# The last two batches of a switch-head attention layer on one core: DVE adds gated heads with fused multiply-adds, and the last batch is turned, projected and stored per token tile

## What is computed

```python
gl_v = (x @ Ws).reshape(b, t, h, e)
wv = _topk_mask(gl_v, SEL) * jax.nn.sigmoid(gl_v)
xv = jnp.einsum('btd,edk->btek', x, Wv)
v = jnp.einsum('bthe,btek->bhtk', wv, xv)
...
attn = jnp.einsum('bhij,bhjd->bihd', probs, v)
gl_o = (x @ Wd).reshape(b, t, h, e)
mask_o = _topk_mask(gl_o, SEL)
out = jnp.einsum('bthe,bthk,ekd->btd', mask_o, attn, Wo)
```

## Time and profile before

| | us |
|---|---|
| median of 3 executions | 2942.46 |
| lowest, highest | 2939.79, 2952.21 |
| the profiled execution | 2944.26 |
| its span | 2942.5 |
| mean granted TensorE clock | 0.88 |

### The profile page before, as it was taken

One profiled execution on the slowest core, in us unless ns is written; L12 is line 12 of the kernel. 1 busy time (PEld: TensorE's weight loads), 2 busy tenths in 40 slices (PEclk: granted clock), 3 DMA queues, 4 the chain that ended last, 5 costly groups with the idle time before them and its releaser, 6 DMA issues. The chain is left out here.

```text
span 2942.5 us, 31726 instructions
## 1 busy us (share of the span) xinstructions
PE 2436.2 (83%) x10259; PEld 1141.4 (39%) x10259; DVE 1903.9 (65%) x3077; ACT 1689.0 (57%) x2384; POOL 1925.0 (65%) x1920
## 2 busy tenths in 40 slices
PE   5567787877778877755998999999999999999995
PEld 2222333333333332223554454444444444444433
DVE  5798979798888797721332555656565565646554
ACT  1788888888888789920222545454444544444350
POOL 5656577778687778856774027566767574756685
PEclk8678777789787777776999999999999999999996
DMA  2000000000100000164996000000000000000000
GB/s 99 15 1 8 10 15 17 15 17 15 17 15 17 15 10 15 17 113 108 282 261 134 1 1 1 1 15 8 15 8 15 8 1 22 1 8 1 8 1 15
DMA packets 92453, 99.00 MB, mean 34 GB/s; under 512 B 20320, under 2 KB 88032, under 8 KB 92256
## 3 DMA queue, kind: packets, MB, share of 16 engines
q1 hardware_dynamic: 66544, 69.80, 9.0%
q0 software_dynamic: 25712, 26.90, 4.7%
HBM read 69.98 MB, written 26.67 MB: 33 GB/s over the span
## 5 line engine op out<-in xcount | busy, mean ns | idle before, releaser
L944 POOL TENSOR_TENSOR TT<-TT,SS 128x512 f32<-128x512 f32 x512 | 649.8, 1305 | 218.8 <-ACT SS L874 218.3
L1644 ACT ACTIVATE PR<-S,NM 128x512 f32<-128x512 f32 x512 | 347.0, 683 | 492.7 <-DVE NM L1812 492.6
L1812 DVE TENSOR_REDUCE NM<-S 128x2 f32<-128x1024 f32 x256 | 313.0, 1223 | 294.7 <-PE S L1548 293.9
L447 PE MATMUL OB<-TT,VAL 128*17 128x512 f32 x1024 | 339.8, 766 | 53.6 <-ACT TT L882 53.5
L700 DVE TENSOR_SCALAR TT<-SC 128x1024 f32<-128x1024 f32 x256 | 311.6, 1217 | 81.4 <-PE SC L426 49.1
L949 POOL DMA_INDIRECT slot_tokens<-TID,IDX x256 | 258.9, 1011 | 138.0 <-issue 79.2
L702 DVE SCALAR_TENSOR_TENSOR SS<-SC,TT 128x1024 f32<-128x1024 f32 x256 | 313.6, 1225 | 20.6 <-issue 1.8
L1577 PE MATMUL OT<-TT,VN 128*64 128x512 f32 x1024 | 278.8, 623 | 20.7 <-ACT TT L1650 16.8
L1548 PE MATMUL S<-TT 64*128 64x512 f32 x1024 | 292.1, 646 | 0.7 <-ACT TT L1613 0.7
L1559 PEld LDWEIGHTS TP<-ident,PR 128*128 128x128 f32 x2048 | 227.1, 141 | 149.8 <-issue 121.1
L1559 PE MATMUL TP<-ident,PR 128*128 128x128 f32 x2048 | 275.5, 278 | 10.1 <-DVE TT L1817 8.7
(11 more groups left out here) (272 smaller groups left out, 4168.2 us busy)
## 6 DMA issues: line engine op xcount, KB each, us to landing
TT<-w_gu SPq DMA_DIRECT2D x64, 384.0 KB, 3.9
TT<-w_dn SPq DMA_DIRECT2D x64, 128.0 KB, 4.2
XL<-x SPq DMA_DIRECT2D x8, 512.0 KB, 4.0
rows<-XL SPq DMA_DIRECT2D x8, 512.0 KB, 10.2
slot_tokens<-TID,IDX POOLq DMA_INDIRECT x256
TT<-w_dn SPq DMA_DIRECT2D x64, 64.0 KB, 4.9
XS<-stream SPq DMA_DIRECT2D x8, 512.0 KB, 3.8
out<-XS SPq DMA_DIRECT2D x8, 512.0 KB, 2.9
```

Source lines behind the costliest of these rows:

```text
L447: ins = pe.matmul(OB[r:r + DH0 + 1, :], values_of[:, mt, h, :], TT[:, h % RING, mt, :], start=(mt == 0), stop=(mt == NT - 1))
L944: ins = pool.tensor_tensor(tt[:, mt, :], tt[:, mt, :], ss[:, mt, :], ALU.add)
L1644: act.activation(PR[s % 2][h2][:], S[s % 2][:, h2, :], ACT.Exp, bias=NM[:, s % 2, h2:h2 + 1], accum_out=SM[:, pair % 2, j, h2:h2 + 1]).the ...
L1812: dve.tensor_reduce(NM[:, s % 2, :], S[s % 2][:], AX, ALU.max, negate=True).then_inc(sems["peak"], 1)
```

## The change

It has three parts.

1. **Lending.** DVE takes both heads of pair 3 of batch 6 over from POOL. `lend` 0 and 1 stand at steps 8 and 9 of run 15: for each token tile and expert one `scalar_tensor_tensor` of 128x64 that multiplies a head's output with one column of choices and adds it to GO, so 20 for each head. POOL's `gate` for that pair is gone, and in its place POOL waits for `lent` and counts `gadd` up by two. PE waits for `lent` ahead of `turn_out2` 0.
2. **Fused gating of the last batch.** DVE's even heads of pairs 1 and 2 are added with 20 such instructions each instead of 4 products (L1752) and an addition (L1756). For pair 0 the 4 products stay. Of pair 3 DVE now takes both heads, and POOL none.
3. **Tile by tile at the end.** In place of `join`, three `turn_out2` and four `product_out2` there is `finish` for each token tile: DVE adds the 10 fused instructions of pair 3 and joins the tile (128x320), PE turns it in 3 transposes, ACT copies it (128x384), PE makes the product one tile later in its queue, DVE adds the residual, and SP stores 128 KB. Ahead of the first tile PE has 4 products of 128x512 into a bank that nobody reads.

```diff
--- before.py
+++ after.py
@@ -1179,15 +1179,14 @@
 OUT_2_LATE = table((0, 12, 1, "turn_out2", 0), (0, 13, 1, "turn_out2", 1), (0, 13, 2, "turn_out2", 2),
                    (0, 14, 1, "product_out2", 0), (0, 14, 2, "product_out2", 1), (0, 15, 2, "product_out2", 2),
                    (1, 0, 1, "product_out2", 3))
-OUT_2_TAIL = table((0, 4, 3, "join", 0), (0, 4, 3, "turn_out2", 0), (0, 4, 3, "turn_out2", 1), (0, 4, 3, "turn_out2", 2),
-                   (0, 4, 4, "product_out2", 0), (0, 4, 4, "product_out2", 1), (0, 4, 4, "product_out2", 2),
-                   (0, 4, 4, "product_out2", 3))
+OUT_2_TAIL = table(*[(0, 4, 3, "finish", j) for j in range(NT + 1)], *[(0, 4, 4, "residual", j) for j in range(NT)])
 HEADS_1 = table((0, 7, 1, "spread", 0), (0, 11, 1, "spread", 1), (0, 15, 1, "spread", 2), (1, 3, 1, "spread", 3),
                 (0, 7, 2, "heads1", 0), (0, 11, 2, "heads1", 1), (0, 15, 2, "heads1", 2), (1, 3, 2, "heads1", 3))
 HEADS_2 = table((0, 7, 2, "set_down", 0), (0, 11, 2, "set_down", 1), (0, 15, 2, "set_down", 2), (1, 3, 2, "set_down", 3),
                 (0, 8, 2, "heads2", 0), (0, 12, 2, "heads2", 1), (1, 0, 2, "heads2", 2), (1, 4, 2, "heads2", 3),
                 (0, 9, 3, "gate", 0), (0, 13, 3, "gate", 1), (1, 3, 3, "gate", 2), (1, 7, 3, "gate", 3))
-HEADS_2_TAIL = HEADS_2[:8] + table((0, 9, 3, "gate", 0), (0, 13, 3, "gate", 1), (1, 0, 3, "gate", 2), (1, 4, 3, "gate", 3))
+HEADS_2_TAIL = HEADS_2[:8] + table((0, 9, 3, "gate", 0), (0, 13, 3, "gate", 1), (1, 0, 3, "gate", 2))
+LEND = table((1, 8, 3, "lend", 0), (1, 9, 3, "lend", 1))
 
 
 def timetable():
...
@@ -1200,6 +1199,8 @@
 
     for r, (kind, b) in enumerate(RUNS):
         put(r, HEADS_1 if kind == 1 else HEADS_2 if b < B - 2 else HEADS_2_TAIL, b)
+        if (kind, b) == (2, B - 2):
+            put(r, LEND, b)
         if r + 1 == TAIL:
             put(r, OUT_2_LATE, b - 1)
             continue
...
@@ -1344,13 +1345,16 @@
                 sp.dma_start(X[b][:], x_b[b]).then_inc(sems[f"x_in{b}"], 16)
             for dst, src in loads_later:
                 sp.dma_start(dst, src).then_inc(sems["weights_later"], 16)
-            for b in range(B):
+            for b in range(B - 1):
                 sp.wait_ge(sems["x4"], b + 1)
                 sp.dma_start(out_b[b], X[b % XN_RING][:]).then_inc(sems["out_st"], 16)
                 if b + XN_RING < B:
                     sp.wait_ge(sems["out_st"], 16 * (b + 1))
                     sp.dma_start(X[b % XN_RING][:], x_b[b + XN_RING]).then_inc(sems[f"x_in{b % XN_RING}"], 16)
-            sp.wait_ge(sems["out_st"], 16 * B)
+            for j in range(NT):
+                sp.wait_ge(sems["row_out"], j + 1)
+                sp.dma_start(out_b[B - 1][:, j, :], X[(B - 1) % XN_RING][:, j, :]).then_inc(sems["out_st"], 16)
+            sp.wait_ge(sems["out_st"], 16 * (B - 1 + NT))
 
         @block.tensor
         def _(pe):
...
@@ -1488,26 +1492,40 @@
                 ins.then_inc(sems["item_d"], 1)
 
             def turn_out2(v, c, b):
-                last = b == B - 1
-                bank = free_bank(c) if last else item(v, "free_d")
-                if last and c == 0:
-                    pe.wait_ge(sems["joined"], 1)
-                elif c == 0:
-                    pe.wait_ge(sems["gadd"], v.next("gadd", H1))
+                bank = item(v, "free_d")
+                if c == 0:
+                    pe.wait_ge(sems["gadd"], v.next("gadd", H1) - (2 if b == B - 2 else 0))
+                    if b == B - 2:
+                        pe.wait_ge(sems["lent"], 2)
                 lo = min(c * P, SV - P)
                 for j in range(NT):
-                    ins = pe.transpose(bank[:, j * P:(j + 1) * P], (GL_POOL if last else GO)[:, j, lo:lo + P], ident[:])
+                    ins = pe.transpose(bank[:, j * P:(j + 1) * P], GO[:, j, lo:lo + P], ident[:])
                 ins.then_inc(sems["item_d"], 1)
 
-            def product_out2(v, j, b):
-                bank = free_bank(3 + j) if b == B - 1 else item(v, "free_d")
-                if b == B - 1 and v.all_due("free_d"):
-                    pe.wait_ge(sems["free_d"], v.value + 3)
+            def out2_into(bank, j):
                 for c in range(3):
                     r = 0 if c < 2 else 3 * P - SV
                     ins = pe.matmul(bank[:, 0:D], AT2[r:P, c, j * P:(j + 1) * P], o2[r:P, c, :],
                                     start=(c == 0), stop=(c == 2))
-                ins.then_inc(sems["item_d"], 1)
+                return ins
+
+            def product_out2(v, j, b):
+                out2_into(item(v, "free_d"), j).then_inc(sems["item_d"], 1)
+
+            def finish(v, i, b):
+
+                if i == 0:
+                    for _ in range(4):
+                        pe.matmul(free_bank(6), ident[:], q2[:, 0, :], start=True, stop=True)
+                if i < NT:
+                    pe.wait_ge(sems["joined"], i + 1)
+                    for c in range(3):
+                        lo = min(c * P, SV - P)
+                        ins = pe.transpose(free_bank(i)[:, c * P:(c + 1) * P], GL_POOL[:, i, lo:lo + P], ident[:])
+                    ins.then_inc(sems["turned_j"], 1)
+                if i > 0:
+                    pe.wait_ge(sems["down_j"], i)
+                    out2_into(free_bank((4, 5, 6, 0)[i - 1]), i - 1).then_inc(sems["done_j"], 1)
 
             def spread(v, pair, b):
 
...
@@ -1613,6 +1631,12 @@
                     act.activation(dst(i, b), src(), ACT.Copy, scale=scale).then_inc(sems["free_a"], 1)
                 return run
 
+            def finish(v, i, b):
+                if i < NT:
+                    act.wait_ge(sems["turned_j"], i + 1)
+                    act.activation(AT2[:, :, i * P:(i + 1) * P], S[i // 2][:, i % 2, 0:3 * P].rearrange("p (c n) -> p c n", c=3),
+                                   ACT.Copy).then_inc(sems["down_j"], 1)
+
             def absorb(v, i, b):
                 for g in range(2):
                     act.wait_ge(sems["wide"], g + 1)
...
@@ -1738,34 +1763,60 @@
 
             def turn_out2(v, c, b):
                 dve.wait_ge(sems["item_d"], v.next("item_d"))
-                dve.tensor_copy(AT2[:, c, :], free_bank(c) if b == B - 1 else BK[:]).then_inc(sems["free_d"], 1)
+                dve.tensor_copy(AT2[:, c, :], BK[:]).then_inc(sems["free_d"], 1)
+
+            def add_gated(acc, pair, h2, b, j):
+                for e in range(SE):
+                    part = acc[:, j, e * DH1:(e + 1) * DH1]
+                    ins = dve.scalar_tensor_tensor(part, AH[pair % 2][:, j, h2, :], MO[b % 2][:, j, 2 * pair + h2, e:e + 1], part,
+                                                   ALU.mult, ALU.add)
+                return ins
 
             def gate(v, pair, b):
 
                 if b < B - 1:
                     return
-                gl = GL_DVE.rearrange("p j (e d) -> p j e d", e=SE)
-                gt = GT_DVE.rearrange("p j (e d) -> p j e d", e=SE)
-                h = 2 * pair
-                dve.drain()
-                for j in range(NT):
-                    ins = dve.tensor_tensor((gt if pair else gl)[:, j], AH[pair % 2][:, j, 0, :].unsqueeze(1).to_broadcast([P, SE, DH1]),
-                                            MO[b % 2][:, j, h, :].unsqueeze(2).to_broadcast([P, SE, DH1]), ALU.mult)
-                if pair:
+                dve.drain()
+                if pair == 0:
+                    for j in range(NT):
+                        dve.tensor_tensor(GL_DVE[:, j].rearrange("p (e d) -> p e d", e=SE),
+                                          AH[0][:, j, 0, :].unsqueeze(1).to_broadcast([P, SE, DH1]),
+                                          MO[b % 2][:, j, 0, :].unsqueeze(2).to_broadcast([P, SE, DH1]), ALU.mult)
+                else:
+                    for j in range(NT):
+                        add_gated(GL_DVE, pair, 0, b, j)
+                dve.drain()
+
+            def lend(v, h2, b):
+
+                if h2 == 0:
+                    dve.wait_ge(sems["gadd"], H1 * (B - 1) - 2)
+                for j in range(NT):
+                    ins = add_gated(GO[:], PAIRS1 - 1, h2, b, j)
+                dve.drain()
+                dve.sem_inc(sems["lent"], 1)
+
+            def finish(v, i, b):
+
+                if i == NT:
+                    return
+                if i == 0:
+                    dve.wait_ge(sems["gadd"], H1 * B - 2)
                     dve.drain()
-                    ins = dve.tensor_tensor(GL_DVE, GL_DVE, GT_DVE, ALU.add)
-                ins.then_inc(sems["own"], 1)
-
-            def join(v, i, b):
-                dve.wait_ge(sems["gadd"], H1 * B)
-                dve.drain()
-                dve.tensor_tensor(GL_POOL, GL_POOL, GL_DVE, ALU.add).then_inc(sems["joined"], 1)
+                for h2 in range(2):
+                    add_gated(GL_DVE, PAIRS1 - 1, h2, b, i)
+                    dve.drain()
+                dve.tensor_tensor(GL_POOL[:, i], GL_POOL[:, i], GL_DVE[:, i], ALU.add).then_inc(sems["joined"], 1)
+
```

(23 more changed lines are left out.)

## The result

| | before | changed |
|---|---|---|
| median of 20 executions, us | 2952.57 | 2962.83 |
| lowest, highest | 2939.79, 2966.45 | 2952.34, 2971.06 |
| profiled execution, its span | 2944.26, 2942.5 | 2962.43, 2960.7 |

The ratio is 1.0031, with a 95% interval of 1.0018 to 1.0044: 9 us slower, 5 to 13. That is within the 0.5% named ahead, but the forecast was 4 us faster, and both 2962.83 and 2942.46 x 1.0031 = 2951.6 lie above the range.

A forecast was written before the change was run, and what follows sets the result against it. The prediction took POOL's queue up to the join and a serial PE chain behind it as the bound. Its terms, +4.0 - 1.0 + 2.3 - 9.4 = -4.1 us, gave 2940.2 us profiled (2938.4 off the median), range 2927 to 2949.

The forecast's parts named there:

- 1, lending: Both `lend`s on DVE, 7.7 us each, turn PE's 10 us stall into two of 8 us: +4.0 us.
- 2, pair 1: Fused gating of pair 1 in batch 7 takes 4.6 us instead of 5.56: -1.0 us.
- 3, pair 2: Fused gating of pair 2 beside POOL makes the stretch to pair 3 8.4 us instead of 6.14: +2.3 us.
- 4, the end: Tile-by-tile end, bounded by PE at half clock, takes 22.7 us instead of 32.1: -9.4 us.
- the price of a fused instruction: One 128x64 `scalar_tensor_tensor` on DVE costs 0.135 us alone and 0.385 beside POOL's mixing.
- Two for each POOL operation: During POOL's mixing, DVE fits two fused instructions per POOL operation, at a pace of 0.77 us.
- rival 2: DVE gets one instruction in per POOL operation, `lend` 0 takes 16.4 us: +4.9 us, 2947.4; chance 0.20.
- the point of loss: The change becomes a loss from some 0.58 us for a fused instruction on.
- a rival for the changed one alone: Idle products and a tighter queue bring PE's clock up at the end: -10.1 us, 2932.4; chance 0.20.
- What was said of the signs: PE's wait for POOL gone, `lend`s of 7 to 9 us, PE idle about 8 us twice, 3.2 us products ending the span.

The follow-up runs named there:

- probe_fused: Changed kernel with the ten fused instructions of each end tile in four forms (unchanged, constant multiplier, other result buffer, plain addition): ten took 2.21 us unchanged.
- base2: The kernel before, unaltered, profiled a second time: its end from pair 3 on took 26.29 us, against 32.13 in the first profile.
- lendonly: The kernel before with the lending alone, pairs 1 to 3 and the end as before: ratio 1.0033 to before.
- base_warm: The kernel before with 15 idle products ahead of PE's wait for the joined tile: median 2953.56 us, ratio 0.9992 to before.
- oldform_warm2: Changed kernel with lending and gating of pairs 1 and 2 as four products and an addition, 10 idle products instead of 4: 2945.16 us, ratio 0.9952.
- endonly_warm: The kernel before with only the tile-by-tile end, pair 1 gated by products and an addition, 10 idle products: 2949.83 us, ratio 0.9971.
- oldform: Changed kernel with lending and gating of pairs 1 and 2 as four products and an addition, 4 idle products kept: ratio 0.9972 to before.
- endonly: The kernel before with only the tile-by-tile end, no lending, old form for pairs 1 and 2, 4 idle products: ratio 0.9979 to before.

## Why the prediction was wrong

By its own terms, against before's first profile as the forecast was made:

| term | forecast | measured |
|---|---|---|
| 1, lending | +4.0 | +8.55 |
| 2, pair 1 | -1.0 | -0.16 |
| 3, pair 2 | +2.3 | +3.52 |
| 4, the end | -9.4 | -8.95 |
| sum | -4.1 | +2.96 |

- **The step that failed is the price of a fused instruction**, 0.135 us alone and 0.385 beside POOL. I took the L735 row for the first. Its operations have no column of multipliers and weren't measured in a long series; probe_fused gives 0.16 for such a one and 0.22 with the column. "Two for each POOL operation" was then too many: 20 in 9.42 us at POOL's pace of 0.73 are 1.5. The measured 0.47 us stays far from rival 2 (16.4 us for a `lend`) and below the 0.58 us that I gave as the point of loss. That point was too high by the forecast's own terms: the 40 instructions of the two `lend`s all stand beside the mixing, and 0.1 us more for each of them already uses up the 4.1 us. That puts it at some 0.49, an estimate.
- **Term 1** is 4.55 over: 1.7 and 1.4 from the two `lend`s, 0.4 from pair 0's products, and 1.5 from the way from those products to `turn_out2` 0, 6.33 us (2893.78 to 2900.11) instead of 4.85; 0.4 came back behind it. I gave PE's clock 0.9 back for a shorter pause. There are now two pauses, and PE's first transposes behind each took 1.97 us, where they take 1.09 in the earlier trace rows: that way got longer, while the one from `turn_out2` 0 to AH1 got 1.3 shorter (3.88 us).
- **Terms 2 and 3** missed by the same price: 5.60 us instead of 4.6, and 8.56 instead of 7.3 (5 or 6 instructions between POOL's four products instead of 8, and about 13 behind its addition at 0.2 us each). That one instruction stands behind POOL's whole addition was right.
- **Term 4** was right in mechanism and size, 23.2 for 22.7, with products of 3.06 us. A tile takes DVE 2.69 us, not 2.1. That shows as a first transpose 3.6 us after AH3 instead of 3.0, and as PE's 1.79 us wait for the second tile; products and store a little shorter than forecast hid half of it.
- **A second fault, in the base and not in a term**: the sum was made against one profile, whose end at 0.50 is the dearest of the four profiles of that end (32.1 us; the others, in base2, lendonly and base_warm with its idle products, 25.4 to 26.3). I kept 0.50 for both kernels and put the rise as a rival for the changed one alone. Where it rises in both, the end by tiles gains 6.8 us and not 9, and the balance is +8.8 instead of +3.0, of which most of the 2.8 in AH1 to AH2 goes with the clock there. That the forecast's term 4 came out at -8.95 is therefore in part luck: both first profiles had their end at 0.50.
- What was said of the signs held: PE's wait for POOL gone, two idle stretches of 8 to 10 us, copies and joins beside the products. `lend` at 9.4 us lay between the forecast's 7 to 9 and rival 2's 12.

**The version that beats both** keeps the end by tiles and drops the fused form wherever POOL works. oldform_warm2 is 0.9952 [0.9931, 0.9972], some 14 us under before, and endonly_warm 0.9971. The medians put oldform_warm2 4.7 us below endonly_warm, and in the earlier pair oldform 3.2 below endonly. That is what the rival named for it (1.5 us or more), against my 1 us. But by the tails the warm pair is 0.8 us apart in the other order, the intervals overlap, and the unchanged part of endonly_warm's profile was 4.6 us longer (2804.9 for 2800.3). Whether the lending in the old form gains anything is open.

## What to carry to other kernels

Price a fused instruction by its own kind, with its operands, beside the neighbour it will have: here one of 64 elements cost 0.22 us alone and 0.47 beside POOL, and four long products and one addition beat twenty of them. When two engines hinder each other, ask who loses: here the short instructions of the critical engine paid alone, and with long ones the other engine paid too. And profile a serial PE chain behind a pause twice before pricing its replacement: its clock is part of what the old code costs, and one profile shows one draw of it.

## What the runs showed of the hardware

- A column of multipliers, with POOL idle, adds 0.06 us to a fused DVE instruction of 128x64 (2.21 against 1.60 for ten).
- POOL's four products and addition took 2.83 and 2.88 us beside fused instructions of DVE and 3.78 and 3.95 beside DVE's long products and additions. The latter are before's; the addition is in the earlier trace rows, and this is the row of the products:

```profile
2905.09 3.78 POOL L1912 TENSOR_TENSOR GT<-AH,MO 128x320 f32<-128x320 f32 x4 [6.57 <-DVE AH L1844]
```

- The same program's last stretch was granted 0.50 throughout in one execution and 0.86 in another. With idle products over the wait before it, it was 1.00.
